# First attention stage: projections in turns over two PSUM banks, one order of steps on all engines, and attention loops aligned to instruction slot 0

## The reference

```python
kv_c = x @ W_kv                      # rank 32
kv_c = kv_c * rsqrt(mean(kv_c * kv_c) + EPS) * g_kv
q_c = x @ W_q                        # rank 64
k_content, v = heads(kv_c @ W_kdec, 8), heads(kv_c @ W_vdec, 8)
q_content = heads(q_c @ W_qdec, 8)
k_rope, q_rope = heads(x @ W_krope, 32), heads(q_c @ W_qrope, 32)
q_rope, k_rope = apply_rope(q_rope, cos, sin), apply_rope(k_rope, cos, sin)
scores = einsum('bhqd,bhkd->bhqk', [q_content, q_rope], [k_content, k_rope]) / sqrt(40)
attn = softmax(where(causal, scores, -inf))      # 16 heads, 256 queries, 256 keys
out = merge(attn @ v) @ W_o
```

## Time and profile before

| what | value |
|---|---|
| runs | 3691.65 us median of 3 (3690.67 to 3692.14) |
| the profiled execution | 3689.71 us |
| its span, first to last instruction | 3687.9 us |
| TensorE clock granted, mean share | 0.902 |
| busy: PE / PEld / DVE / ACT / POOL | 2932.4 / 2107.1 / 2055.7 / 1573.2 / 1326.9 us |
| first attention stage (copies of x from 54.8 to 656.7) | about 600 us |
| second attention (n = 2), copies of x | 871.0 to 1215.4 us |
| third attention (n = 4), copies of x | 1520.3 to 1887.0 us |
| "5l", "5h", n = 6, copies of x | 1947.5 to 2248.4, 2319.3 to 2709.3, 2741.5 to 3423.8 us |

### The profile page before, as it was taken

How to read it: one execution, slowest core, us unless ns; L and a number is a source line. 1 busy time by engine, 2 the same in 40 slices (tenths; PEclk the granted TensorE clock), 3 DMA queues, 4 the chain that set the end, 5 groups by cost and what they waited for, 6 DMA issues and landing times. The chain is left out here.

```text
span 3687.9 us, 76319 instructions
## 1 busy us (share of the span) xinstructions
PE 2932.4 (80%) x22136; PEld 2107.1 (57%) x22137; DVE 2055.7 (56%) x7855; ACT 1573.2 (43%) x4312; POOL 1326.9 (36%) x1531
## 2 busy tenths in 40 slices
PE   5777777696878456488868996899989999999656
PEld 4555555363555234366646664566656666666546
DVE  3555555465888512577764556555555455444464
ACT  1323333223555223355535663455546665566310
POOL 3555555004777221566632332222222222222110
PEclk7999999797999778799989997899989999999765
DMA  2000000122000111100000000000000000000000
GB/s 55 1 1 1 0 1 1 45 63 72 2 1 1 53 46 43 41 2 1 1 30 1 0 0 0 1 0 0 0 22 1 1 0 0 1 0 0 3 0 23
DMA packets 41273, 47.49 MB, mean 13 GB/s; under 512 B 6224, under 2 KB 30921, under 8 KB 40777
## 3 DMA queue, kind: packets, MB, share of 16 engines
q1 hardware_dynamic: 38992, 40.97, 3.9%
q0 software_dynamic: 2048, 4.20, 0.4%
HBM read 35.03 MB, written 10.12 MB: 12 GB/s over the span
## 5 line engine op out<-in xcount | busy, mean ns | idle before, releaser
L1690 POOL TENSOR_TENSOR a_sm<-a_sm,a_top 128x512 f32<-128x512 f32 x576 | 587.3, 1040 | 377.4 <-DVE a_top L1503 377.3
L1614 ACT ACTIVATE a_pr<-a_sm 128x512 f32<-128x512 f32 x576 | 355.7, 627 | 306.9 <-POOL a_sm L1690 189.5
L1503 DVE CUSTOM_DVE_ANT_0 a_sm<-bank,cst 128x256 f32<-128x256 f32 (+1 forms) x1024 | 302.8, 353 | 143.5 <-PE bank L1377 109.9
L735 ACT ACTIVATE a_pr<-a_sm,a_top 128x256 f32<-128x256 f32 (+1 forms) x512 | 227.5, 446 | 243.5 <-DVE a_top L602 234.6
L1391 PE MATMUL bank<-cst,a_pr 128*128 128x128 f32 x2304 | 320.3, 284 | 0.6 <-ACT a_pt L1624 0.4
L602 DVE CUSTOM_DVE_ANT_0 a_sm<-bank,cst 128x256 f32<-128x256 f32 (+1 forms) x512 | 157.8, 355 | 271.0 <-PE bank L494 251.0
L1391 PEld LDWEIGHTS bank<-cst,a_pr 128*128 128x128 f32 x2304 | 270.9, 146 | 29.7 <-issue 20.3
L1511 DVE COPY a_pt<-bank 128x512 f32<-128x512 f32 x288 | 197.8, 687 | 140.9 <-PE bank L1391 139.0
L1624 ACT ACTIVATE a_pt<-bank 128x512 f32<-128x512 f32 x288 | 169.2, 587 | 117.0 <-PE bank L1391 113.1
L494 PE MATMUL bank<-a_kx,a_q 128*128 128x512 f32 (+1 forms) x512 | 202.5, 499 | 3.1 <-issue 3.1
L735 ACT ACTIVATE a5h_pr<-bank,a5h_top 128x256 f32<-128x256 f32 x256 | 119.0, 469 | 163.8 <-DVE a5h_top L607 131.7
(11 more groups left out here) (455 smaller groups left out, 6927.3 us busy)
## 6 DMA issues: line engine op xcount, KB each, us to landing
f_spread<-gate_rows SPq DMA_DIRECT2D x16, 512.0 KB, 7.6
W<-in_l_w SPq DMA_DIRECT2D x2, 2048.0 KB, 10.0
x_sorted<-p_zero SPq DMA_DIRECT2D x4, 768.0 KB, 5.5
f_xin<-x_sorted SPq DMA_DIRECT2D x12, 256.0 KB, 2.9
y_sorted<-f_yout SPq DMA_DIRECT2D x10, 256.0 KB, 2.3
X<-in_x SPq DMA_DIRECT2D x4, 512.0 KB, 7.2
a_bias<-bias_rows SPq DMA_DIRECT2D x1, 2048.0 KB, 8.0
out_x<-X SPq DMA_DIRECT2D x8, 256.0 KB
```

Source lines behind the costliest of these rows:

```text
L735: ins = act.activation(pr[s % R][:, h * kw:(h + 1) * kw], src[:, h * kw:(h + 1) * kw], ACT.Exp, bias=top[:, qt, h0 + h:h0 + h + 1], scale= ...
L1503: ins = dve.tensor_tensor_reduce(sm[j][:, m * kw:(m + 1) * kw], sbank[j][:, m * kw:(m + 1) * kw], mk, 1.0, 3.0e38, ALU.add, ALU.min, top[: ...
L1614: act.activation(pr[j][:, :], sm[j][:, :], ACT.Exp, scale=-1.0).then_inc(S["probs"], 1)
L1690: pool.tensor_tensor(whole, whole, top[:, qt, a:a + m].unsqueeze(2).to_broadcast([P, m, kw]), ALU.subtract).then_inc(S["shifted"], 1)
```

## The change

The first attention gets `lanes = 2`: its steps take turns in bank 7 and in score bank 0, and each bank has a semaphore of its own (`step_out0`, `step_out1`) for its readings. A step in bank 7 waits for the step two places before it; a step in bank 0 does so too, and for mask 0 of the same slot. The scores of the next slot wait for the last step that used bank 0. The work at a tile's end leaves bank 0: `project` uses bank 3, `denominators` and `repeat_turn` keep banks 1 and 2. The order of the slot becomes the same on all engines: step 3 comes before `repeat_turn` and `project` on TensorE, steps 2 and 3 come directly after mask 3 on VectorE (with `recip` between), and GpSimd does the steps between the shifts. The other stages keep `lanes = 1` and their order.

```diff
-            with eng.Fori(1, BATCH // 2) as i:
+            with eng.bass.Fori(1, BATCH // 2, engines=[eng.engine], head_slot={eng.engine: 0}) as i:
...
-        YB, DB, RB = sbank[0:3]
+        lanes = steps.lanes
+        y_bank, d_bank, r_bank = (0, 1, 2) if lanes == 1 else (3, 1, 2)
+        YB, DB, RB = sbank[y_bank], sbank[d_bank], sbank[r_bank]
+        LANE = [PRE, sbank[0]]
...
                 pe.wait_ge(S["masked"], total(i, 2 * U, 4 * s) + CREDIT)
+                if lanes == 2:
+                    pe.wait_ge(S["step_out1"], total(i, NS, b * NS // 2 + NS // 2 + q * NS // NQ // 2) + CREDIT)
...
-                pe.wait_ge(S["step_out"], (max(j - len(FIRST) + 1, 0) if first else seq * NS + j) + CREDIT)
+                if not first:
+                    pe.wait_ge(S[steps.out_of(j)], steps.nth_out(seq, j) - 1 + CREDIT)
+                    if j % lanes:
+                        masks_done(i, b * NQ - NQ + j * NQ // NS, 0)
...
-                steps.pe(pe, core, B, S, FIRST[j % len(FIRST)] if first else PRE, j, b % 2, seq).then_inc(S["step_mm"], 1)
+                steps.pe(pe, core, B, S, FIRST[j % len(FIRST)] if first else LANE[j % lanes], j, b % 2, seq).then_inc(S["step_mm"], 1)
...
                 for e in ending(i, s, LD):
                     denominators(i, s, e)
+                if in_loop(i) and lanes == 2:
+                    steps_in(i, s, 3)
                 for e in ending(i, s, LRT):
                     repeat_turn(i, s, e)
+                if lanes == 2:
+                    for e in ending(i, s, LY):
+                        project(i, s, e)
...
                     mask(i, s, 3)
-                for e in ending(i, s, LY):
-                    residual(i, e)
+                    if lanes == 2:
+                        steps_in(i, s, 2)
+                if lanes == 1:
+                    for e in ending(i, s, LY):
+                        residual(i, e)
                 for e in ending(i, s, LD):
                     recip(i, e)
+                if in_loop(i) and lanes == 2:
+                    steps_in(i, s, 3)
                 for e in ending(i, s, LRT):
                     norm(i, e)
+                if lanes == 2:
+                    for e in ending(i, s, LY):
+                        residual(i, e)
...
                     for j in range(4):
                         shift(i, s, j)
+                        if lanes == 2 and j:
+                            steps_in(i, s, j - 1)
...
+    def out_of(self, j):
+        return f"step_out{j % self.lanes}"
+
+    def nth_out(self, seq, j):
+        return seq * (self.count // self.lanes) + j // self.lanes + 1
```

More of the change, by code:

```diff
@@ L1277, in narrow_stage @@
         S = {}
-        for s in ("x_copied", "step_mm", "step_out", "rope_added", "k_ready", "scores", "masked", "shifted", "probs", "turned",
+        for s in ("x_copied", "step_mm", "step_out0", "step_out1", "rope_added", "k_ready", "scores", "masked", "shifted", "probs", "turned",
                   "turned_out0", "turned_out1", "turned_out2", "turned_out3", "values", "gathered", "dens", "recip", "repeated", "rep_turned",
@@ L1360, in scores @@
                     if isinstance(i, int) and i == 0 and s == 0:
-                        pe.wait_ge(S["step_out"], NS + CREDIT)
+                        pe.wait_ge(S["step_out0"], NS // lanes + CREDIT)
                 pe.wait_ge(S["masked"], total(i, 2 * U, 4 * s) + CREDIT)
+                if lanes == 2:
+                    pe.wait_ge(S["step_out1"], total(i, NS, b * NS // 2 + NS // 2 + q * NS // NQ // 2) + CREDIT)
                 pe.wait_ge(S["residual"], total(i, 4, begun(s, LY)) + CREDIT)
@@ L1399, in values @@
                 if q == 0:
-                    pe.wait_ge(S["step_out"], total(i, 2 * NS, (s // NQ + 1) * NS) + CREDIT)
+                    per_lane = NS // lanes
+                    pe.wait_ge(S[steps.out_of(NS - 1)], total(i, 2 * per_lane, (s // NQ + 1) * per_lane) + CREDIT)
                 if q in (0, hd.first_late):
@@ L1418, in project @@
             def project(i, s, e):
-                masks_done(i, s, 0)
+                masks_done(i, s, y_bank)
                 pe.wait_ge(S["normed"], 4 * i + e + 1 + CREDIT)
@@ L1427, in denominators @@
             def denominators(i, s, e):
-                masks_done(i, s, 1)
+                masks_done(i, s, d_bank)
                 pe.wait_ge(S["gathered"], 4 * i + e + 1 + CREDIT)
@@ L1435, in repeat_turn @@
             def repeat_turn(i, s, e):
-                masks_done(i, s, 2)
+                masks_done(i, s, r_bank)
                 pe.wait_ge(S["repeated"], 4 * i + e + 1 + CREDIT)
@@ L1479, in slot @@
                     turn(i, q, 3)
-                if in_loop(i):
+                if in_loop(i) and lanes == 1:
                     steps_in(i, s, 3)
@@ L1553, in step @@
                     if first:
-                        dve.wait_ge(S["step_out"], j + CREDIT)
-                    steps.dve(dve, core, B, S, FIRST[j % len(FIRST)] if first else PRE, j, b % 2, seq).then_inc(S["step_out"], 1)
+                        dve.wait_ge(S[steps.out_of(j)], steps.nth_out(0, j) - 1 + CREDIT)
+                    steps.dve(dve, core, B, S, FIRST[j % len(FIRST)] if first else LANE[j % lanes], j, b % 2, seq
+                              ).then_inc(S[steps.out_of(j)], 1)
             steps.before(dve, core, B, S)
@@ L1636, in step @@
                     if first:
-                        act.wait_ge(S["step_out"], j + CREDIT)
-                    steps.act(act, core, B, S, FIRST[j % len(FIRST)] if first else PRE, j, b % 2, seq).then_inc(S["step_out"], 1)
+                        act.wait_ge(S[steps.out_of(j)], steps.nth_out(0, j) - 1 + CREDIT)
+                    steps.act(act, core, B, S, FIRST[j % len(FIRST)] if first else LANE[j % lanes], j, b % 2, seq
+                              ).then_inc(S[steps.out_of(j)], 1)
             for j in range(NS):
@@ L1706, in _, with steps_in @@
                 steps.pool(pool, core, B, S, j, 0, 0)
+            def steps_in(i, s, place):
+                b = s // NQ
+                for j in steps_at(s, place):
+                    steps.pool(pool, core, B, S, j, (b + 1) % 2, 2 * i + b + 1)
             def slot(i, s):
@@ L1714, in slot @@
                 if in_loop(i):
-                    b, q = divmod(s, NQ)
-                    for j in at_quad[q]:
-                        steps.pool(pool, core, B, S, j, (b + 1) % 2, 2 * i + b + 1)
-                    if q == NQ - 1:
-                        copy_x(i, b + 2)
+                    for place in range(4) if lanes == 1 else (3,):
+                        steps_in(i, s, place)
+                    if s % NQ == NQ - 1:
+                        copy_x(i, s // NQ + 2)
             all_quads(pool, slot)
@@ L1729 @@
     content = False
+    lanes = 1
     def alloc(self, sb, sem, B, S):
@@ L1801, in pool @@
             return
-        pool.wait_ge(S["step_out"], 3 * seq + j + 1 + CREDIT)
+        pool.wait_ge(S[self.out_of(j)], self.nth_out(seq, j) + CREDIT)
         dst = B["q"][b] if kind == "q" else B["k"]
@@ L1869 @@
     content = True
+    lanes = 2
     def __init__(self, hd, rkv, F):
```

14 lines of the change are left out of this document (8 added, 6 removed).

## The result

| kernel | median, runs | ratio to before | profiled execution, span |
|---|---|---|---|
| before, beside the changed kernel | 3691.16 us, 3688.4 to 3692.14, 4 | 1 | 3689.71, 3687.9 us |
| changed | 3536.67 us, 3531.82 to 3541.46, 4 | 0.9583 [0.9566, 0.9599] | 3531.82, 3530.0 us |
| changed, again on another occasion | 3537.85 us, 3535.35 to 3540.29, 5 | 0.9595 [0.9582, 0.9608] | span 3537.3 us |

The change saves 154.5 us; 140 were forecast. For the kernel e6 further down, one run of two was disturbed (4508.52 us), so its profiled execution alone is used.

What follows compares the result with a forecast made beforehand. TensorE was taken to idle on the first stage's one-bank projection chain and on VectorE's code fetches at loop back edges. 3689.71 - 74 - 76 + 9 = 3549, predicted as 3551 us for the median, range 3526 to 3605.

Steps and rivals of the forecast that it cites:

- part 1: First stage: two banks for the projections and a new order save 4.6 us per batch element, 74 us in all.
- edges of n = 0: First stage's loop: six taken back edges, read as code fetches on VectorE, cost 9.4 us that alignment removes.
- edges of n = 6: Last attention's loop: back edges cost 269.1 - 6 x 41.3 = 21.3 us, with 41.3 the plain row.
- entries: Loop entries: jumping over the alignment padding, once per loop and engine, loses 9 us, the middle of 0 to 17.
- main case: Whole kernel: the forecast as worked out, 3551 us, chance 0.72; this case alone spans 3526 to 3580.
- head-of-batch wait: First stage, TensorE before a batch element's scores: wait for GpSimd's last rotary sum, 0.15 before and near 0.9 us after.
- T+6.3: First stage's late slot, counted from its turns at T: when GpSimd's last rotary sum ends, against TensorE's T+5.4.
- bound of 85: First stage: upper end of 59 to 85 us for the two banks, if low clock after idle time goes too.
- Part 2: Attention loops on four engines: beginning at slot 0 stops instruction fetches at back edges, saving 76.1 us.
- the bodies don't fit: Rival, VectorE's loops: aligned bodies still fetch at the head, 24 us gained instead of 76; 3603 us, chance 0.14.
- half: Rival, first stage: VectorE or GpSimd late elsewhere, so 37 us gained instead of 74; 3588 us, chance 0.1.
- ring: Rival, first stage: scores wait for VectorE's last multiplication, a closed ring once per slot; 3743 us at 4 us, chance 0.01.

Runs made afterwards that it cites:

- e6: Changed kernel with VectorE's attention loops beginning at slot 37 instead of 0, other engines at 0; 3531.24 us in its profiled execution.
- e2: Changed kernel without the loop alignment, keeping only the two banks and the new order; 3596.67 us, ratio 0.9745.
- e1: Kernel before with only its loops aligned to slot 0, on all engines; 3629.13 us, ratio 0.9836.
- e5: Changed kernel with VectorE's six attention loops beginning at slot 90 instead of 0, other engines at 0; 3575.61 us, ratio 0.9694.
- e4: Changed kernel with two banks and tile-end work in bank 3, but the old order on TensorE, VectorE and GpSimd; 3716.24 us, ratio 1.0063.
- e3: Changed kernel with all projections back in bank 7, keeping the new order and tile-end work in bank 3; 3670.29 us, ratio 0.9943.
- e9: Kernel of e8 with TensorE's wait for the last rotary sum moved behind the first quad's four content matmuls; 3496.97 us, ratio 0.9481.
- e7: Changed kernel with VectorE's loops alone aligned, the other engines' loops opened as before; 3530.46 us, ratio 0.9579.
- e8: Changed kernel with VectorE reading the slot's second projection before its copy, and GpSimd's rotary sums moved to match; 3524.66 us, ratio 0.9558.

## Why the prediction was right, and where its terms were off

| term | forecast | measured | by |
|---|---|---|---|
| part 1, sixteen batch elements | 74 | 91 | e2 |
| edges of n = 0 | 9.4 | 3.4 alone, none with part 1 | e1, e2 |
| edges of n = 2 | 13.1 | 11.6 + 1.4 of the entry | stages |
| edges of n = 4 | 32.3 | 31.3 | stages |
| edges of n = 6 | 21.3 | 27.7 | stages |
| entries | -9 | -4.4 | entry elements |
| between n = 2 and n = 4 | 0 | -4.6 | copies of x |

The main case held; that the total came within 14 us is in part luck, since its errors had different signs. **Part 1** went by the slot that the prediction worked out: the remaining 1.07 us, T+3.20, T+5.58, the free scores. The head-of-batch wait was mis-sized, 1.57 for 0.9 on average. In the slot shown (turns at T = 247.77) GpSimd's sum runs from 253.07 to 253.81, T+6.04, and the scores start at 254.42, 0.61 after its end; I had let them start with it. (The T+6.3 written there doesn't follow from the terms beside it: 3.84 + 1.04 + 0.72 is 5.60, and 6.3 needs a second sum of 0.72 on the way, which I didn't write down. In the profile that sum lies between the shifts 2 and 3.) TensorE was there at T+4.99, not T+5.4. Against that stands the term that I left to the upper bound, the clock. Per batch element the waits shrank by 3.7 us and the busy time by 1.8, 5.5 in all; the 4.6 forecast were waiting alone. Of the 1.8 at most 1.3 are the clock: 30.7 us of the twelve elements before ran at 1.2 GHz, none now, and 30.7/2/12 = 1.3. Where the other 0.5 comes from isn't shown. The bound of 85 was too low by 6. Two reasons can be named: 9.4 us stood under the edges instead (below), and the first two elements with what leads up to them gained 13.4 us (84.8 to 71.4), for which 9.2 were counted.

**Part 2** was right in n = 2 and 4 by the mechanism given, and e5 and e6 put its border where the pieces of 128 have it. The step that failed is the 9.4 for n = 0: a difference between elements with and without an edge was read as the price of a fetch, because the fetch was there. e1 takes the fetch away and keeps 1.1 of 1.6 us, so the fetch was worth 3.4 us and not 9.4; and in e2, with part 1, it costs nothing. The errors cancel in part: 9.4 too much here, 17 too little in part 1, 83 for 91 together. The 41.3 of n = 6, taken as the floor, wasn't one; elements of 40.9 give some 6 us more.

**The rivals.** That the bodies don't fit is excluded by the empty transfers and by e5, where they really don't. The first stage gained more than the forecast, not half. The ring that makes it slower exists: e4 has it, since there the order isn't changed along with the banks. In the changed kernel the last multiplication ends 0.43 us before the scores start.

## What to carry to other kernels

A second buffer helps only if the engine that empties it does so in an order that frees the first one in time; change the banks and the order on all engines together (e3 and e4 against e1 and the changed kernel). Before a step at a loop's edge is priced as a fetch, see whether the clock in it differs from its neighbours', and whether the engine that fetches would wait there anyway. When waits of 1 to 2 us are taken from TensorE, take the busy time of the same matmuls at both clocks into the sum: here up to a quarter of what came back was the clock (1.3 of 5.7 us per batch element), and nearly half in e9.

## What the hardware showed that was not expected

- VectorE's loop bodies are free at their back edges up to slot 384 of their block (347 instructions at slot 37, 285 at 90) and refetch from 387 on (e5, e6). A refetch that nothing hides leaves VectorE idle at the head for 2.1 to 3.1 us per turn in n = 2 (e2, e5).
- With slot 0 there is idle time at the entry of a loop: 3.1 us on TensorE, 3.0 on VectorE, 2.2 on ScalarE, at one entry each, and only the first two cost time. TensorE's goes when only VectorE's loops are aligned (e7), VectorE's at slots 37 and 90 (e6, e5).
- In e8 the clock fell to 1.2 GHz behind each of the six waits of 2.05 to 2.10 us in front of the scores, and behind none of the six of 1.87 to 1.90. Shortened to 0.95 us, they left it at 1.00 in all twelve elements (e9). The 1.1 us of waiting taken away brought 1.8.
